# Earlier batch fronts and an earlier reciprocal in a two-layer attention and mixture-of-experts kernel

## The chip, the cores and the metric

The kernel runs on one core of a Trainium2 chip. The time is device microseconds of one execution, and the figure for the kernel before is the median of three executions: 1724.65 us (1723.31 to 1725.45). The profile is of one of them.

## The reference, cut to what matters

The input `x` has 4 batches of 1024 tokens of width 128. Two layers run one after the other, each as `x = x + layer(layernorm(x))`.

```
# layer 1: pre-norm attention, 16 heads of 8, causal, then a GELU MLP (128 -> 512 -> 128)
h = layernorm(x); q, k, v = h @ Wqkv; q, k = rotate(q), rotate(k)
a = softmax(where(causal, q @ k.T / sqrt(8), -inf)); x = x + (a @ v) @ Wo
x = x + gelu(layernorm(x) @ W1 + b1) @ W2 + b2
# layer 2: attention, 16 heads of 8, not causal, then 8 experts of which each token takes 2
q, k = rope(x @ Wq + bq), rope(x @ Wk + bk); v = x @ Wv + bv
ao = softmax(q @ k.T / sqrt(8)) @ v
x1 = layernorm(x + ao @ Wo + bo)
p = top2(softmax(x1 @ Wg + bg)), renormalised
out = layernorm(x1 + sum over the 2 experts of p_e * (gelu(x1 @ W1_e + b1_e) @ W2_e + b2_e))
```

## The kernel before, in words

Each engine has its own program, and semaphores tie the programs together. Both attentions are one class, `Attention`, with `a` = 1 (causal) and 2. The 64 pairs of batch and head are worked in 16 groups of 4 heads (`NG` = 16, `HG` = 4), so groups 0 to 3 are batch 0, 4 to 7 batch 1, and so on.

A group has two kinds of work. A **chunk** is one block of scores, made on TensorE (L536) only so that VectorE can take the row maxima of it (`row_max`, L623); there are 24 chunks in a group of the first attention and 32 in one of the second. A **unit** makes scores again (L568), now with the row maximum subtracted by extra rows of the operands, ScalarE takes the exponential (L677), and a **values** step (L592) multiplies it with V. There are 24 units in a group of the first attention and 32 in one of the second. A column of ones in V gives the sum of each row, and the sums leave with the outputs (`o_sums`, stored to DRAM as `heads_out`).

The order is written out once by `attention_plan` and every engine walks it: in group i, unit by unit, about one chunk is placed behind each unit, and those chunks belong to groups i+1 (chunks 6 and up) and, near the end, i+2 (chunks 0 to 5). All chunks share two PSUM buffers (`CHUNK_BUFS` = 2), so TensorE can be at most two chunks ahead of VectorE, and since the units stand between the chunks in the same program, whatever holds VectorE's row maxima soon holds TensorE and ScalarE.

When the four groups of batch b are done, the softmax sums of that batch are turned into reciprocals by three steps: SyncE reads the sums from DRAM into `sums_in` (`load_sums`, L469), in its turn for group i = 4(b+1), behind the row loads of a later group (`load`, L458, eight transfers); VectorE takes the reciprocal (`reciprocals`, L480); SyncE stores it (`store_reciprocals`, L473) in its turn for group i+1, again behind eight row loads. VectorE does its step in group i+1 (groups 5, 9, 13), two thirds of the way through the units (unit 16 of 24, unit 21 of 32). The step of the last batch stands elsewhere. Each SyncE turn i waits for all scores of group i before it issues the row loads.

In the second attention the **front** of a batch (output projection, layernorm, gate logits) is woven into a later group, `FRONT_GROUP[q]`: 7, 11 and 15 for batches 0, 1 and 2. SyncE loads its data before turn `FRONT_GROUP[q] - 1` (`load_front`, L982 to L985, three transfers for each half, after waiting for the stored reciprocals). GpSimd multiplies heads by reciprocals (`first_scale`, L1160), TensorE projects at `PRODUCT_UNIT` (L1329), VectorE adds and takes moments (L1572, L1555), ScalarE normalises 9 and 11 units later, TensorE transposes at `TURN_UNIT` (L762) and makes logits at `LOGITS_UNIT` (L1342). These TensorE steps borrow the chunk buffers. Group `SORT_GROUP` (12) holds the sort of tokens by expert for batches 0 and 1, and GpSimd scatters the tokens (L1191) from there on. Before turn 14 SyncE also loads the first three experts' weights (L1004) and the first sorted rows (L1016). After the attention come the expert blocks.

## Time and profile before

| | |
|---|---|
| median of three | 1724.65 us |
| the profiled execution, its own time | 1725.45 us |
| its span | 1723.6 us |
| TensorE busy | 1453.4 us (84%) |
| VectorE busy | 1275.0 us (74%) |
| ScalarE busy | 1164.6 us (68%) |
| first attention, group 0 to 15 | about 122 to 600 us of the span |
| second attention, group 0 to 15 | about 805 to 1471 us of the span |

In the names below PE is TensorE, PEld its weight load, DVE VectorE, ACT ScalarE, POOL GpSimd, and SPq the issuing queue of SyncE. An engine's idle time costs only where that engine, or one that waits for it, sets the pace.

### The profile page before, as it was taken

To read this page: it belongs to the slowest core of one execution; us is meant where nothing else is said; L and a number is where in the kernel's file an instruction comes from. 1 tells how busy PE (TensorE), PEld (TensorE's weight loads), DVE (VectorE), ACT (ScalarE), POOL (GpSimd) and SP (SyncE) were. 2 spreads that over 40 slices of the span, in tenths; PEclk is the share of its full clock that TensorE was granted. 3 is DMA by queue.
4 is the path that set the end of the run, shared out by engine and by line. 5 is a ranking of instruction groups with operands and counts; after the bars stand their busy time and mean duration, and the time that the engine had idled before them with its cause. 6 is when DMAs were issued, how large, how long until landed. Compare 5 with 4: busy or idle time off the path is not lost.

```text
span 1723.6 us, 39125 instructions
## 1 busy us (share of the span) xinstructions
PE 1453.4 (84%) x15249; PEld 668.5 (39%) x15249; DVE 1275.0 (74%) x1978; ACT 1164.6 (68%) x2370; POOL 370.9 (22%) x409
## 2 busy tenths in 40 slices
PE   4759999998989878856999999899988999898980
PEld 2323444444444355511222222222222223688870
DVE  6877787777777146569999999899989994261354
ACT  4627777777777755512989999789977998433341
POOL 3410000000000056420000000200021431267771
PEclk9959999999999989975999999999999999999995
DMA  3523241212111134440000102000200130566873
GB/s 115 189 84 113 94 139 56 78 53 85 57 46 36 62 102 129 128 140 8 33 33 33 39 34 71 33 32 34 71 32 34 64 124 14 156 189 212 265 227 104
DMA packets 132777, 152.94 MB, mean 89 GB/s; under 512 B 13744, under 2 KB 107824, under 8 KB 132336
## 3 DMA queue, kind: packets, MB, share of 16 engines
q1 hardware_dynamic: 122480, 123.43, 23.0%
q0 software_dynamic: 10112, 27.01, 4.2%
q8 instruction: 120, 1.97, 0.5%
q14 instruction: 65, 0.53, 0.1%
HBM read 90.90 MB, written 63.46 MB: 90 GB/s over the span
## 4 chain that ended last, share of the span: by engine, by line
PE 46%; DVE 25%; ACT 9%; issue 8%; DMA 6%; SPq 4%; POOL 2%; ACTq 0%; POOLq 0%; DVEq 0%
DVE row_max L623 20%; PE bank L592 16%; PE banks L568 9%; PE banks L536 6%; ACT probs L677 4%; PE banks L1386 4%; PE banks L1396 4%; DMA qk_parts<-parts 2%; SPq L486 2%; DMA q_work<-max_T 2%; PE banks L576 1%; ACT max_T L668 1%; ACT o_sums L688 1%; PE banks L323 1%; POOL pair_out L1202 1%
## 5 line engine op out<-in xcount | busy, mean ns | idle before, releaser
L623 DVE TENSOR_REDUCE row_max<-banks 128x2 f32<-128x1024 f32 (+3 forms) x896 | 938.1, 1101 | 130.7 <-PE banks L542 75.4
L677 ACT ACTIVATE probs<-banks 128x512 f32<-128x512 f32 (+3 forms) x1792 | 879.8, 552 | 175.8 <-PE banks L576 84.3
L592 PE MATMUL bank<-probs,v_ones 128*32 128x256 f32 (+3 forms) x7168 | 534.1, 375 | 20.0 <-ACT o_sums L688 16.8
L536 PE MATMUL banks<-k_work,q_work 48*128 48x512 bf16 (+3 forms) x1792 | 365.6, 380 | 75.8 <-DVE row_max L623 59.4
L568 PE MATMUL banks<-q_work,k_work 51*128 51x512 bf16 (+3 forms) x1792 | 384.5, 371 | 41.3 <-DMA q_work<-max_T 25.7
L715 POOL DMA_DIRECT2D heads_out<-o_sums x64 | 35.5, 555 | 1051.5 <-ACT o_sums L688 1051.5
L568 PEld LDWEIGHTS banks<-q_work,k_work 51*128 51x128 bf16 x1792 | 102.5, 93 | 407.7 <-ACT probs L677 316.7
L592 PEld LDWEIGHTS bank<-probs,v_ones 128*32 128x32 f32 x7168 | 147.1, 109 | 253.2 <-ACT probs L677 187.1
L536 PEld LDWEIGHTS banks<-k_work,q_work 48*128 48x128 bf16 x1792 | 95.0, 96 | 142.1 <-DVE row_max L623 108.4
L1962 ACT ACTIVATE rope<-banks,expert 128x256 f32<-128x256 f32 x184 | 72.0, 473 | 111.9 <-PE banks L1386 111.9
L1386 PE MATMUL banks<-rope,expert 128*128 128x256 f32 x368 | 93.2, 399 | 15.3 <-issue 7.7
L1396 PE MATMUL banks<-expert,rope 128*128 128x128 f32 x736 | 91.5, 278 | 0.6 <-DVE k_work L1699 0.6
L323 PE MATMUL banks<-hT,w_qk 128*128 128x512 f32 x128 | 69.5, 677 | 22.3 <-ACT hT L386 12.8
L1396 PEld LDWEIGHTS banks<-expert,rope 128*128 128x128 f32 x736 | 87.7, 195 | 0.8 <-ACT rope L1962 0.8
L576 PE MATMUL banks<-later_keys_T,half_ident 64*128 64x64 bf16 (+1 forms) x1024 | 80.3, 213 | 0.0
L1386 PEld LDWEIGHTS banks<-rope,expert 128*128 128x128 f32 x368 | 69.8, 200 | 25.2 <-issue 14.2
L542 PE MATMUL banks<-later_keys,half_ident 64*128 64x64 bf16 (+1 forms) x1024 | 75.2, 214 | 0.0
L1191 POOL DMA_INDIRECT sorted_in<-v_all,slots x64 | 67.6, 1056 | 20.9 <-issue 19.2
L668 ACT ACTIVATE max_T<-banks 12x1024 bf16<-12x1024 bf16 x32 | 32.1, 1004 | 54.9 <-PE banks L552 54.9
L1691 DVE COPY rope<-banks 128x256 f32<-128x256 f32 x46 | 19.4, 421 | 60.8 <-PE banks L1375 60.8
L542 PEld LDWEIGHTS banks<-later_keys,half_ident 64*128 64x128 bf16 x1024 | 55.7, 101 | 16.3 <-issue 3.2
L688 ACT ACTIVATE o_sums<-bank 128x512 f32<-128x512 f32 x64 | 38.9, 608 | 32.5 <-PE bank L592 32.5
(204 smaller groups left out, 1156.7 us busy)
## 6 DMA issues: line engine op xcount, KB each, us to landing
expert<-expert_rows SPq DMA_DIRECT2D x46, 578.0 KB, 4.0
qk_parts<-parts SPq DMA_DIRECT2D x64, 256.0 KB, 3.4
heads_out<-o_sums POOLq DMA_DIRECT2D x64, 256.0 KB, 4.3
q_work<-qk_parts SPq DMA_DIRECT2D x64, 128.0 KB
k_work<-qk_parts SPq DMA_DIRECT2D x64, 128.0 KB
sorted_in<-zeros SPq DMA_DIRECT2D x4, 1472.0 KB, 12.4
parts<-sorted_in SPq DMA_DIRECT2D x22, 256.0 KB, 4.7
probs<-in_x SPq DMA_DIRECT2D x16, 256.0 KB, 4.0
```

What stands on the lines that cost most here:

```text
L323: pe.matmul(bank[QK_BANK + u % QK_BANKS], w_qk[a][:, i, :], hT[:, :], start=True, stop=True).then_inc(s["qk"], 1)
L536: last = pe.matmul(to[:, par, 0:width], q[r:r + M0, pair, qt * P:(qt + 1) * P], k[r:r + M0, pair, kh * G:kh * G + width], start=True, stop ...
L542: last = pe.matmul(to[:, par, width - P + c0:width], half_ident[r:r + HALF, half, :], later_keys[r:r + HALF, half, c0:P], start=False, sto ...
L568: last = pe.matmul(to[par][:, 0:G - c0], k[r:r + M1, pair, kt * P:(kt + 1) * P], q[r:r + M1, pair, qh * G + c0:(qh + 1) * G], start=True, ...
L576: last = pe.matmul(to[par][:, 0:c1], half_ident[r:r + HALF, half, :], later_keys_T[r:r + HALF, half, 0:c1], start=False, stop=half == 1)
L592: last = pe.matmul(bank[7][32 * j:32 * j + 32, c0 + part * w:c0 + (part + 1) * w], v_ones[i % QB][:, kt, j, :], prob_slots[:, (e + j) % RI ...
L623: dve.tensor_reduce(row_max[:, qt, 2 * pair:2 * pair + 2, kh], self.buf_of("chunk", g, c)[:, :, 0:width], AX.X, ALU.max).then_inc(s["chunk ...
L677: act.activation(prob_slots[:, e % RING, 0:width], banks46[:, e % EXP_BANKS, 0:width], ACT.Exp, scale=SCALE).then_inc(s["exps"], 1)
L1191: pool.indirect_dma_start(xs_d[section], bass.IndirectOffsetOnAxis(slots[:, section, i, tile:tile + 1], 0), x1s[:, JOINED * section + tile ...
L1386: last = pe.matmul(hidden(m, f), expert[:, m % W_BUFS, f * P:(f + 1) * P], xsT[:, m % 2, :], start=True, stop=True)
L1396: last = pe.matmul(bank[Y_BANK][:, side * P:(side + 1) * P], h_block[:, m % 2, f, side * P:(side + 1) * P], expert[:, m % W_BUFS, FF + f * ...
L1962: act.activation(h_block[:, m % 2, f, :], hidden(m, f), ACT.Gelu, bias=expert[:, m % W_BUFS, 2 * FF + f:2 * FF + f + 1]).then_inc(end["gel ...
```

## The change

Two things change. VectorE's `reciprocals` step is no longer taken at two thirds of groups 5, 9 and 13 of both attentions, but ahead of the first chunk of these groups. And in the second attention the fronts of batches 0 and 1 go from groups 7 and 11 to groups 6 and 10, five units later in the group (product at 11 for 6, turn at 25 for 20, logits at 30 for 25); the front of batch 2 stays in group 15 at its units. `SORT_GROUP` follows from 12 to 11. SyncE's `load_front` stays before turns 6, 10 and 14, since `FRONT_GROUP[q]` now stands where `FRONT_GROUP[q] - 1` stood; the three expert loads go from turn 14 to turn 13.

```diff
-FRONT_GROUP = tuple(HG * q + 2 * HG - 1 for q in range(FIRST))
+FRONT_GROUP = tuple(HG * q + HG + 2 for q in range(JOINED)) + (NG - 1,)
 SORT_GROUP = FRONT_GROUP[JOINED - 1] + 1
-PRODUCT_UNIT, TURN_UNIT, LOGITS_UNIT, RANKS_UNIT = (6, 6, 1), (20, 20, 13), (25, 25, 17), 8
+PRODUCT_UNIT, TURN_UNIT, LOGITS_UNIT, RANKS_UNIT = (11, 11, 1), (25, 25, 13), (30, 30, 17), 8
...
                 for i in range(-1, NG):
+                    if i % HG == 1 and i > 1:
+                        self.reciprocals(dve, i // HG - 1)
                     for what, ahead, n in self.order:
-                        if what == "unit" and i % HG == 1 and i > 1 and n == self.nu * 2 // 3:
-                            self.reciprocals(dve, i // HG - 1)
...
             def load_ahead(i):
                 for q in range(FIRST):
-                    if i == FRONT_GROUP[q] - 1:
+                    if i == min(FRONT_GROUP[q], NG - 2):
                         for k in range(HALVES):
                             load_front(q, k)
-                if i == NG - 2:
+                if i == NG - 3:
                     sp.wait_ge(mid["x_out"], 16 * GROUPS)
                     sp.wait_ge(rows_made, 16 * len(made))
                     for m in range(W_BUFS - 1):
                         load_expert(m)
+                if i == NG - 2:
                     for i in range(2):
                         load_rows(0, i)
```

VectorE's program around the start of group 5 of the first attention, before (the row maxima of group 4's turn and group 5's run together in the count, 6 + 17):

```order
L641 CAST max_parts<-max_rest 128x32
L643 TENSOR_TENSOR max_parts<-max_rest,max_parts 128x32
L623 TENSOR_REDUCE row_max<-banks 128x2 x23
L480 RECIPROCAL sums_rcp<-sums_in 128x128
L623 TENSOR_REDUCE row_max<-banks 128x2
```

The same place after the change:

```order
L641 CAST max_parts<-max_rest 128x32
L643 TENSOR_TENSOR max_parts<-max_rest,max_parts 128x32
L623 TENSOR_REDUCE row_max<-banks 128x2 x6
L480 RECIPROCAL sums_rcp<-sums_in 128x128
L623 TENSOR_REDUCE row_max<-banks 128x2 x18
```

The reciprocal has moved ahead of 17 row maxima; behind it now stand all chunks that VectorE does in group 5's turn up to the maxima step. The five other places are alike.

TensorE's program in group 6 of the second attention (+ is what is new there; L1330 is L1329 of before), with the place in group 7 from which the first product is gone:

```order
@@ -2846,4 +2846,6 @@
 L592 MATMUL bank<-probs,v_ones 32x256 x4
 L568 MATMUL banks<-q_work,k_work 128x512 x2
+L1330 MATMUL banks<-w_o,headsT 128x128 x4
+L1330 MATMUL banks<-w_o,hT 128x128 x4
 L536 MATMUL banks<-k_work,q_work 128x512 x2
 L592 MATMUL bank<-probs,v_ones 32x256 x4
@@ -2924,6 +2928,4 @@
 L592 MATMUL bank<-probs,v_ones 32x256 x4
 L568 MATMUL banks<-q_work,k_work 128x512 x2
-L1329 MATMUL banks<-w_o,headsT 128x128 x4
-L1329 MATMUL banks<-w_o,hT 128x128 x4
```

The two projections stand behind unit 11 of group 6 and ahead of the next chunk of it; they stood behind unit 6 of group 7.

SyncE's program around turn 13 of the second attention:

```order
@@ -467,4 +467,16 @@
 L458 DMA k_work<-qk_parts 16x1x2048
 L469 DMA sums_in<-heads_out 128x1x128
+L1003 TENSOR_LOAD block_expert
+L1003 ISA x2
+L1004 ISA
+L1004 DMA expert<-expert_rows 128x1156
```

One of three such expert loads is shown; they now follow the read of the sums, and stood behind the six transfers of `load_front` one turn later.

## Rows read from the trace of the kernel before

**Rows 1.** The page's first part: busy us (share), instructions of each engine.

```profile
PE 1453.4 (84%) x15249; PEld 668.5 (39%) x15249; DVE 1275.0 (74%) x1978; ACT 1164.6 (68%) x2370; POOL 370.9 (22%) x409
```

**Rows 2.** Busy time by stretch: us, engines, granted clock (PEclk), DMA share, GB/s.

```profile
270.80:302.10 31.30, 28.93 (x424) 12.93 (x424) 23.77 (x31) 22.55 (x51) 1.50 (x4) 0.89 0.22 68
333.10:361.80 28.70, 26.05 (x424) 12.14 (x424) 22.91 (x30) 22.52 (x51) 1.48 (x3) 1.00 0.18 60
1043.00:1082.00 39.00, 37.10 (x394) 10.20 (x392) 37.49 (x38) 35.73 (x67) 1.48 (x3) 1.00 0.25 78
```

**Rows 3.** Timeline of VectorE, groups 5, 9, 13 of both attentions: start, length, [idle before].

```profile
272.20 1.22 DVE L623 TENSOR_REDUCE row_max<-banks 128x2 f32<-128x1024 f32 x1 [1.36 <-PE banks L542]
...
393.31 4.97 DVE L623 TENSOR_REDUCE row_max<-banks 128x2 f32<-128x1024 f32 x5 [1.37 <-PE banks L542]
...
513.16 4.97 DVE L623 TENSOR_REDUCE row_max<-banks 128x2 f32<-128x1024 f32 x5 [1.31 <-PE banks L542]
...
1003.68 2.49 DVE L623 TENSOR_REDUCE row_max<-banks 128x2 f32<-128x1024 f32 x2 [0.20 <-PE banks L536]
...
1174.12 2.49 DVE L623 TENSOR_REDUCE row_max<-banks 128x2 f32<-128x1024 f32 x2 [0.20 <-PE banks L536]
...
1350.15 2.49 DVE L623 TENSOR_REDUCE row_max<-banks 128x2 f32<-128x1024 f32 x2 [0.20 <-PE banks L536]
```

**Rows 4.** Timeline of SyncE's issues: row loads and reads of the sums.

```profile
402.22 0.71 SPq L469 DMA_DIRECT2D sums_in<-heads_out  x1
...
1004.52 2.61 SPq L458 DMA_DIRECT2D k_work<-qk_parts  x4
...
1177.72 0.56 SPq L469 DMA_DIRECT2D sums_in<-heads_out  x1
```

**Rows 5.** The read of the sums by line: first attention, second attention, all eight.

```profile
L469 SPq DMA_DIRECT2D sums_in<-heads_out x3: 567/708/1007, 280.8 to 517.1; - x3
DMA to landing us min/median/max: 6.0/6.6/8.9
...
L469 SPq DMA_DIRECT2D sums_in<-heads_out x3: 562/567/906, 1007.2 to 1353.7; - x3
DMA to landing us min/median/max: 8.5/9.1/10.3
...
DMA to landing us min/median/max: 2.2/7.5/10.3
```

**Rows 6.** The reciprocal by line: ns min/median/max, first to last start.

```profile
L480 DVE RECIPROCAL sums_rcp<-sums_in x8: 937/941/954, 292.6 to 1476.3; 128x128 f32<-128x128 f32 x8
```

**Rows 7.** Timeline, front loads and first work: SyncE, landing of L985, GpSimd, TensorE.

```profile
1046.84 0.41 SPq L473 DMA_DIRECT2D reciprocals<-sums_rcp  x1
1058.69 0.59 SPq L985 DMA_DIRECT2D xa<-z_d  x1
1228.92 0.59 SPq L985 DMA_DIRECT2D xa<-z_d  x1
...
DMA to landing us min/median/max: 4.6/5.0/5.8
...
1085.02 1.27 POOL L1160 TENSOR_TENSOR hT<-heads_in 128x512 f32<-128x512 f32 x1
...
1054.92 0.39 PE L568 MATMUL banks<-q_work,k_work 51*128 51x512 bf16 x2
1088.88 1.16 PE L1329 MATMUL banks<-w_o,headsT 128*128 128x128 f32 x8
1225.36 0.39 PE L568 MATMUL banks<-q_work,k_work 51*128 51x512 bf16 x2
```

**Rows 8.** Timeline of TensorE in group 7, at unit 16.

```profile
1110.57 0.64 PE L592 MATMUL bank<-probs,v_ones 128*32 128x256 f32 x8 [1.84 <-ACT o_sums L688]
```

**Rows 9.** Timeline of TensorE at the first expert block, after an idle stretch.

```profile
1477.66 3.62 PE L1386 MATMUL banks<-rope,expert 128*128 128x256 f32 x8 [5.22 <-DVE rope L1691]
...
1482.06 1.96 PE L1386 MATMUL banks<-rope,expert 128*128 128x256 f32 x8 [0.56 <-issue]
```

## The prediction, made before the changed kernel ran

> **What bounds the kernel now.** I read the page's busy times first, then the busy time by stretch, then the timeline of VectorE and TensorE at the places that the diff names, and last the issues and landings of the transfers there. TensorE is busy 84% of the span, VectorE 74% [rows 1]; the shares hide that the two attentions have different limits. A group of the first attention takes 28.7 us when the granted clock is 1.00, with TensorE busy 26.0 of it and VectorE 22.9: TensorE and ScalarE set the pace, VectorE has some spare time. A group of the second takes 39 us with VectorE busy 37.5 and TensorE 37.1 [rows 2]: VectorE sets the pace and nothing has room. In both, the chunks tie the engines: two buffers, so a wait on VectorE reaches TensorE after two chunks, and through the units ScalarE. Nothing behind can be done early, so a wait there is paid in full.
>
> The reader is to see for each touched step when its data lands against when its engine gets to it. Before, the reciprocals stand late enough that no wait shows in the six groups.
>
> **Step 1, the reciprocal ahead of the first chunk.** The instruction itself costs 0.94 us wherever it stands [rows 6]. What it waits for is the read of the sums, and that is issued late: SyncE first waits for all scores of the group before, then issues eight row loads. In the second attention the last of these are still being issued at 1004.5, and the read goes out at 1007.2 [rows 4, 5]. It lands 8.5 to 10.3 us after its issue, in the first attention 6.0 to 8.9 us [rows 5]. VectorE would start on the first chunk of the same group at 1003.7 [rows 3]. So the wait is there in all six places.
>
> *First attention.* The issues are at 280.8, 402.2 and 517.1, with 6.0, 6.6 and 8.9 us to land; the sum of the three landing times is 1200.1 + 21.5 = 1221.6, whichever delay belongs to which. VectorE's first chunks start at 272.20, 393.31 and 513.16, together 1178.7 [rows 3 to 5]. The difference is 42.9 us. The reciprocal comes on top, 3 x 0.94 = 2.8, because the place it leaves had spare time and gives nothing back. From 45.7 I take 0.3 for each place, since the first chunks of a group, which now wait ready in the buffers, follow each other a little more closely. That makes 45 us. TensorE can work on for two chunks and three units, then it stands too, so the whole is on the path.
>
> *Second attention.* Issues at 1007.2, 1177.7 and 1353.7, together 3538.6, and 8.5 + 9.1 + 10.3 = 27.9 to land, so 3566.5; first chunks at 1003.68, 1174.12 and 1350.15, together 3528.0 [rows 3 to 5]. The difference is 38.5 us, about 12 to 14 for each place. The 0.94 us is paid here and saved at unit 21, where VectorE also sets the pace: nothing.
>
> Both together 83.5 us. The bound below is a read that lands as fast as the fastest of the eight, 2.2 us [rows 5]; then the waits shrink by 21.5 + 27.9 - 6 x 2.2 = 36.2 to 47.3. Above, the landings might be slower by a microsecond or so each, where transfers that stood elsewhere come near: about 90. I take the landings as measured, because SyncE's program up to that read is the same and the same row loads are ahead of it. The Trainium skill (DMA: Bandwidth & Descriptors, Anatomy of one DMA) gives a transfer a fixed cost of about 2.0 us and 436 GB/s for its bytes, for one that has nothing ahead of it; by it alone these 64 KB would land in some 2.2 us, and step 1 would cost 47. The trace agrees for the fastest read only and has 6.0 to 10.3 us for the six that matter, so I give that rule a rival's chance below and no more.
>
> **Step 2, the fronts in groups 6 and 10.** The loads of a front stand in the same turn of SyncE as before, but the consumer comes a group earlier. In group 6: the reciprocals' store is issued at 1046.8 behind eight row loads, SyncE waits for its landing, and the last of the six front loads is issued at 1058.7. L985 takes up to 5.8 us to land: 1064.5. GpSimd's second product takes 1.27 us: 1065.8 [rows 7]. Without a wait TensorE would end unit 11 of that group at 1055.3 and start the second half's projection a microsecond later, at 1056.3 (in group 7 the first half took 1.16 us) [rows 7]. So it would stand for 9.5 us. In group 10 unit 11 ends at 1225.7, the last load is issued at 1228.9 and lands some 4.9 us later (the four are 4.6 to 5.8), 1233.8; with 1.27 it is 1235.1 against 1226.7: 8.4 us [rows 7]. Together 17.9 us. Queued behind TensorE's wait are the next chunk and unit, so VectorE and ScalarE stand as well, and it is paid in full. Bounds: 0, if the loads get there in time, and about 25, if the borrowed chunk buffers cost more at the new place than at the old one.
>
> What is won here: in group 7 TensorE waited 1.84 us for `o_sums` at unit 16, since ScalarE had been given the normalising between unit 15 and 17 [rows 8]. Now that comes at units 20 and 22 and is clear of it. Two fronts, 1.8 each: -3.6 us; between 0 and, if turn and logits also fall better, -7. The sort in group 11 is the same work in another group, and the scatter behind it starts a group earlier, with nobody waiting for it in either place. The expert loads in turn 13 go behind the read of the sums and have some 30 us until anyone wants the queue: 0, with a microsecond of slower landing as the worst, which is in the 90 above.
>
> **Step 3, the clock after the waits.** An idle TensorE comes back slowly: after 5.22 us idle the eight matmuls of L1386 took 3.62 us, the next eight 1.96 [rows 9]. That ratio of 1.85 is near that of the levels 1.2 and 2.4 GHz, and the price is 1.7 us. Five places of the second attention and three of the first have longer idle stretches than that. 8 x 1.7 = 13.6 us. Bounds: 0, and 2.6 us each (a group at a granted clock of 0.89 takes 31.3 us where one at 1.00 takes 28.7 [rows 2]), 21 us. The Trainium skill (TensorE: Matmul & The Clock Gate, What's actually happening) says that the default state is throttled and activity releases the throttle; by it each wait is followed by a slow start, as I count it. The trace differs in one way: the first attention falls to 0.89 in groups with no such idle stretch, so some of the slow stretches may only change place there, and without a cost for the three waits of the first attention the sum would be 5.1 us lower.
>
> **The sum.** 45 + 38.5 + 17.9 - 3.6 + 13.6 = 111.4 us. The profiled execution took 1725.45 us, 0.8 above the median of the three: 1725.45 + 111.4 = 1836.9, said as 1837 us.
>
> **The rivals.**
>
> *The fronts' loads are in time.* If the long waits at the start of groups 5 and 9 let the transfers run ahead, group 6 and 10 would find their data. Against it: SyncE's turns are tied to the scores of the same groups, so they are late by the same amount. Without the 17.9 and the two slow starts (3.4) the time is 1815.6, about 1816 us.
>
> *The sums land fast.* While VectorE waits the core is quiet, and the read of 64 KB could land near 2.2 us. For it: the fastest of the eight did [rows 5]. Against it: the row loads ahead of it are the same. Then 36.2 less: 1801 us.
>
> *Faster than before.* The gain of step 2 is real (3.6 us), and if the reciprocals cost nothing and the fronts' data were there, it would be all: 1725.45 - 3.6 = 1722 us. It decides for this side only where the read of the sums has landed by the time VectorE ends the group before, which is some 14 us earlier than any of the six did [rows 3, 5]. I see nothing that would bring that.
>
> *Dearer.* The two chunk buffers are lent to the fronts near the transposes of the row maxima, at the end of the group. If each of turn and logits then waits for a max_T copy, and the clock takes 2.6 us after each wait, it is 1837 + 7 + 8 = 1852 us or a little more.
>
> **How the numbers follow.** The forecast, with step 1, 2 and 3 as worked out: 0.72. Loads of the fronts in time: 0.10. Sums land fast: 0.06. Dearer: 0.09. Faster than before: 0.02; something between that and the others, such as no change because both waits are hidden: 0.01. The range is from 1806 (a forecast without any slow start and with -7 for the relief is 1820; the free fronts with cheaper starts reach down to 1806) to 1856 (the dear case). About 0.2% is what a measurement can tell from no change, 3.5 us. Faster 0.02, same 0.01, slower 0.97.
>
> **What would show it.** In the profile after, VectorE's idle time before the reciprocal (L480) goes to about 120 us over eight places, six of them of 12 to 17 us and ended by the read of the sums. TensorE idles once each in groups 6 and 10 before the projections, for 8 to 10 us, ended by GpSimd's product. The `o_sums` wait of 1.84 us is gone from the groups with a front. Slices with a granted clock below 1 follow each wait in the second attention, which has almost none now. The stretch from the end of the second attention to the end keeps its length. It would be wrong if the waits before L480 were under 8 us each, or if TensorE idled in groups 5, 9 and 13 without the length of the group growing.

## The result and the profile after

| | before | changed |
|---|---|---|
| median | 1723.98 us (4 runs) | 1848.99 us (4 runs, 1845.05 to 1852.15) |
| the profiled execution, its own time | 1725.45 us | 1848.04 us |
| its span | 1723.6 us | 1846.2 us |

The ratio is 1.0728, 95% interval 1.0699 to 1.0758: 125 us slower, where 111 were forecast.

First the page of the changed kernel, busy time by engine:

```profile
PE 1478.0 (80%) x15249; PEld 671.7 (36%) x15249; DVE 1278.0 (69%) x1978; ACT 1164.4 (63%) x2370; POOL 372.5 (20%) x409
```

VectorE and ScalarE did the same work as before [rows 1] to 3 us; TensorE's 25 us more is the same 15249 matmuls, some of them at the lower clock level. Of the 122.6 us that the span grew, VectorE was therefore idle for all but 3, and TensorE for 98. The waits of the changed kernel, who waited for whom, us in total, times, longest:

```profile
DVE sums_rcp L480 <- DMA sums_in<-heads_out: 107.2, 8, 18.8
```

Of these 107.2 us, 18.8 and 0.8 belong to the last batch of each attention, where the kernel before waited about as long (18.7 us for the two). The other six make 87.6. Where VectorE meets them, in group 5 of the first attention and of the second (start, length, [idle before]), which answers to [rows 3]:

```profile
270.45 1.82 DVE L623 TENSOR_REDUCE row_max<-banks 128x2 f32<-128x768 f32 x2 [0.17 <-PE banks L542]
288.78 0.95 DVE L480 RECIPROCAL sums_rcp<-sums_in 128x128 f32<-128x128 f32 x1 [16.51 <-DMA sums_in<-heads_out]
289.65 3.42 DVE L623 TENSOR_REDUCE row_max<-banks 128x2 f32<-128x1024 f32 x3
...
1049.27 3.49 DVE L623 TENSOR_REDUCE row_max<-banks 128x2 f32<-128x1024 f32 x3 [0.40 <-PE banks L536]
1065.24 0.95 DVE L480 RECIPROCAL sums_rcp<-sums_in 128x128 f32<-128x128 f32 x1 [12.48 <-DMA sums_in<-heads_out]
1066.11 3.42 DVE L623 TENSOR_REDUCE row_max<-banks 128x2 f32<-128x1024 f32 x3
1069.96 1.23 DVE L623 TENSOR_REDUCE row_max<-banks 128x2 f32<-128x1024 f32 x1 [0.43 <-PE banks L536]
1071.51 1.22 DVE L623 TENSOR_REDUCE row_max<-banks 128x2 f32<-128x1024 f32 x1 [0.33 <-PE banks L536]
```

The reader is to see two things. The reciprocal starts within 0.1 us of its data, 12 to 17 us after VectorE was free. And behind it the row maxima run on with under a microsecond of idle time: two chunks stood ready in the buffers, and TensorE's slow start shows on VectorE as small gaps only. TensorE at the same place:

```profile
1067.33 0.61 PE L536 MATMUL banks<-k_work,q_work 48*128 48x512 bf16 x2 [12.38 <-DVE row_max L623]
1067.87 1.08 PE L592 MATMUL bank<-probs,v_ones 128*32 128x256 f32 x8
1068.88 0.61 PE L568 MATMUL banks<-q_work,k_work 51*128 51x512 bf16 x2
1069.28 0.64 PE L536 MATMUL banks<-k_work,q_work 48*128 48x512 bf16 x2
1069.85 1.08 PE L592 MATMUL bank<-probs,v_ones 128*32 128x256 f32 x8
1070.86 0.39 PE L568 MATMUL banks<-q_work,k_work 51*128 51x512 bf16 x2
1071.09 0.38 PE L536 MATMUL banks<-k_work,q_work 48*128 48x512 bf16 x2
...
1072.19 0.38 PE L536 MATMUL banks<-k_work,q_work 48*128 48x512 bf16 x2
```

The eight matmuls of L592 take 1.08 us and not 0.64, the pair of L568 0.61 and not 0.39, until 1070.9; so TensorE worked at the lower clock level for about 3.5 us. From one chunk (L536) to the next it took 1.95 and 1.81 us there and 1.10 after, so this start cost it about 1.5 us.

The issue and the landing of the read, first three of the first attention, then of the second (answers to [rows 5]):

```profile
L469 SPq DMA_DIRECT2D sums_in<-heads_out x3: 566/713/1007, 282.2 to 550.7; - x3
DMA to landing us min/median/max: 6.3/6.6/8.5
...
L469 SPq DMA_DIRECT2D sums_in<-heads_out x3: 557/563/567, 1056.5 to 1458.9; - x3
DMA to landing us min/median/max: 8.7/9.0/11.5
```

Now the front in group 6: SyncE's issues, GpSimd, TensorE, VectorE (answers to [rows 7]):

```profile
1109.63 0.42 SPq L473 DMA_DIRECT2D reciprocals<-sums_rcp  x1
1118.90 0.57 SPq L982 DMA_DIRECT2D heads_in<-heads_out  x1
...
1124.91 1.26 POOL L1161 TENSOR_TENSOR headsT<-heads_in 128x512 f32<-128x512 f32 x1 [17.57 <-DMA heads_tok<-z_d]
1127.24 1.26 POOL L1161 TENSOR_TENSOR hT<-heads_in 128x512 f32<-128x512 f32 x1 [1.07 <-DMA xa<-z_d]
...
1126.32 2.04 PE L1330 MATMUL banks<-w_o,headsT 128*128 128x128 f32 x8 [8.31 <-POOL headsT L1161]
1128.56 2.07 PE L1330 MATMUL banks<-w_o,hT 128*128 128x128 f32 x8 [0.20 <-POOL hT L1161]
...
1128.40 0.69 DVE L1573 TENSOR_TENSOR xz<-banks,heads_tok 128x512 f32<-128x512 f32 x1 [9.69 <-PE banks L1330]
1130.67 0.69 DVE L1573 TENSOR_TENSOR yT<-banks,xa 128x512 f32<-128x512 f32 x1 [1.58 <-PE banks L1330]
```

SyncE waits 9 us for the store of the reciprocals, the loads land, GpSimd multiplies, TensorE has stood 8.3 us and then does both projections at the lower clock level, 2.04 us each and not 1.16 and 1.06. VectorE is idle 11.3 us, for TensorE's two projections; in group 7 of the kernel before these two waits were 0.74 us. In group 10 TensorE stood 7.1 and 0.4 us, and the projections took 2.05 and 1.87.

Both stretches by time, groups 5 and 6 of the second attention (from:to, length, PE, PEld, DVE, ACT, POOL busy, granted clock, DMA share, GB/s); [rows 2] has a group of 39 us at 1.00:

```profile
1052.50:1105.50 53.00, 38.91 (x394) 10.28 (x392) 38.51 (x39) 35.87 (x67) 1.48 (x3) 0.87 0.08 28
1105.50:1169.40 63.90, 48.93 (x434) 17.12 (x432) 43.14 (x62) 39.87 (x78) 11.61 (x13) 0.87 0.16 50
```

Measured from one group's last `o_sums` copy to the next, the difference between the two kernels splits like this:

| stretch | before | changed | more |
|---|---|---|---|
| first attention, groups 5, 9, 13 | 88.4 | 136.8 | 48.4 |
| the rest up to the end of the first attention | 510.0 | 509.3 | -0.7 |
| up to the end of group 0 of the second | 248.1 | 249.6 | 1.5 |
| second attention, groups 5, 9, 13 | 119.0 | 163.0 | 44.0 |
| groups 6 to 8 (front of batch 0) | 130.8 | 144.3 | 13.5 |
| groups 10 to 12 (front of batch 1, sort) | 136.4 | 151.5 | 15.1 |
| everything else | 491.1 | 491.8 | 0.7 |

### The profile page after: what moved, and what is told of

The parts are those of the page before. It is cut to its first block, busy times and chain, and to the rows that moved or that the text cites. A ratio compares the mean times of both kernels' runs of the same rounds, so it can differ in the third digit from the quotient of the medians.

```text
span 1846.2 us, 39125 instructions
## 1 busy us (share of the span) xinstructions
PE 1478.0 (80%) x15249; PEld 671.7 (36%) x15249; DVE 1278.0 (69%) x1978; ACT 1164.4 (63%) x2370; POOL 372.5 (20%) x409
## 4 chain that ended last, share of the span: by engine, by line
PE 43%; DVE 21%; issue 9%; DMA 9%; ACT 8%; SPq 7%; POOL 2%; ACTq 0%; POOLq 0%; DVEq 0%
DVE row_max L623 16%; PE bank L592 15%; PE banks L568 9%; PE banks L536 6%; PE banks L1387 4%; PE banks L1397 3%; ACT probs L677 3%; DMA sums_in<-heads_out 3%; SPq L486 3%; SPq L458 2%; DMA qk_parts<-parts 2%; DMA q_work<-max_T 1%; ACT max_T L668 1%; PE banks L576 1%; ACT o_sums L688 1%
## 5 line engine op out<-in xcount | busy, mean ns | idle before, releaser
L592 PE MATMUL bank<-probs,v_ones 128*32 128x256 f32 (+3 forms) x7168 | 546.0, 383 | 16.7 <-ACT o_sums L688 13.6
L536 PE MATMUL banks<-k_work,q_work 48*128 48x512 bf16 (+3 forms) x1792 | 370.2, 387 | 156.2 <-DVE row_max L623 140.9
L568 PE MATMUL banks<-q_work,k_work 51*128 51x512 bf16 (+3 forms) x1792 | 390.1, 376 | 44.9 <-DMA q_work<-max_T 25.7
L568 PEld LDWEIGHTS banks<-q_work,k_work 51*128 51x128 bf16 x1792 | 102.9, 93 | 422.1 <-ACT probs L677 327.2
L592 PEld LDWEIGHTS bank<-probs,v_ones 128*32 128x32 f32 x7168 | 148.8, 110 | 262.6 <-ACT probs L677 189.1
L536 PEld LDWEIGHTS banks<-k_work,q_work 48*128 48x128 bf16 x1792 | 95.4, 97 | 220.2 <-DVE row_max L623 189.9
L480 DVE RECIPROCAL sums_rcp<-sums_in 128x128 f32<-128x128 f32 x8 | 7.6, 953 | 107.2 <-DMA sums_in<-heads_out 107.2
```

Source lines behind the costliest of these rows:

```text
L536: last = pe.matmul(to[:, par, 0:width], q[r:r + M0, pair, qt * P:(qt + 1) * P], k[r:r + M0, pair, kh * G:kh * G + width], start=True, stop ...
L568: last = pe.matmul(to[par][:, 0:G - c0], k[r:r + M1, pair, kt * P:(kt + 1) * P], q[r:r + M1, pair, qh * G + c0:(qh + 1) * G], start=True, ...
L592: last = pe.matmul(bank[7][32 * j:32 * j + 32, c0 + part * w:c0 + (part + 1) * w], v_ones[i % QB][:, kt, j, :], prob_slots[:, (e + j) % RI ...
```

## The experiments

The kernels of one set ran on one chip beside the kernel before. The three sets (e1 to e4, e5 to e8, e9 to e12) met three chips, on which the kernel before took 1815.8, 1732.7 and 1731.1 us. Each result is given against the kernel before of its own set; where an expectation names an absolute time, it stands on 1724 us, and its difference to the kernel before is what counts.

### e1, the reciprocal alone

```diff
 # the kernel before, with
+                    if i % HG == 1 and i > 1:
+                        self.reciprocals(dve, i // HG - 1)
                     for what, ahead, n in self.order:
-                        if what == "unit" and i % HG == 1 and i > 1 and n == self.nu * 2 // 3:
-                            self.reciprocals(dve, i // HG - 1)
```

> The kernel before with the reciprocal alone moved ahead of the first chunk of groups 5, 9 and 13 of both attentions; fronts and expert loads stay. My theory: the six waits for the read of the sums are paid in full and add up with the front's cost, so this alone is worth 88 to 95 us (six waits of 12 to 17 us before L480, 89 us of idle time in the changed kernel, and at most 1 us for each slow start): about 1816 us. Rival (part of the wait is only shifted into the fronts: whatever waits at group 5 is saved at group 6): the sum of the two halves alone is clearly more than 125 us, so this one is over 1830 or the fronts alone cost under 15 us.

1907.33 against 1815.76 us: ratio 1.0508 (1.0453 to 1.0562), 91.6 us more by the medians. VectorE waited 101.6 us before L480, 16.9 of them at the end. As expected.

### e2, the fronts alone

```diff
 # the changed kernel, with
-                    if i % HG == 1 and i > 1:
-                        self.reciprocals(dve, i // HG - 1)
                     for what, ahead, n in self.order:
+                        if what == "unit" and i % HG == 1 and i > 1 and n == self.nu * 2 // 3:
+                            self.reciprocals(dve, i // HG - 1)
```

> The changed kernel with the reciprocal put back at two thirds of the group: only fronts, sort and expert loads are moved. My theory: the late front loads hold TensorE 9 to 11 us in groups 6 and 10, the projections run at the lower clock level after it (about 2 us each) and nothing is won back: 24 to 30 us more than before, about 1751 us. Rival (the forecast's smaller term, 14.3 us net and 3.4 us of slow start): about 1742 us. Rival (the fronts wait only because the reciprocals came late): no wait here, 1720 us.

1839.11 against 1815.76 us: ratio 1.0151 (1.0093 to 1.0208). By the medians 23.4 us more, just under my 24 to 30; the interval (17 to 38 us) holds the forecast's smaller figure of 17.7 as well, so the total alone does not tell the two apart. The trace does, on the point of the wait: TensorE stood 7.3 us before the projections of group 6, and both ran at 2.05 us. The third theory falls: the reciprocals were ready in time here, and the fronts waited all the same. The two halves together are 5.1 + 1.5 = 6.6%, against 6.5% and 7.3% for the whole: they add.

### e3, the read of the sums ahead of the row loads

```diff
 # the changed kernel, SyncE's turn i
                     if i + QB < NG:
                         sp.wait_ge(self.s["scores"], (i + 1) * self.ne)
+                    if i % HG == 0 and i:
+                        self.load_sums(sp, i // HG - 1)
+                    if i + QB < NG:
                         self.load(sp, i + QB)
                     if between:
                         between(i)
-                    if i % HG == 0 and i:
-                        self.load_sums(sp, i // HG - 1)
```

> The changed kernel with one move on SyncE: the read of the sums is issued ahead of the eight row loads (and, in the first attention, of the weight copies) of the same turn instead of behind them. My theory: the read lands late because of what is queued ahead of it, so it is issued 5 to 10 us earlier and lands in 2 to 3 us; VectorE's waits before L480 fall from 12 to 17 us to under 2 us each, and the time falls by about 85 us to 1764 us, with the fronts' 28 us still there. Rival (the landing is slow by itself, 6 to 10 us, whatever is ahead of it): the waits fall only by the earlier issue, 5.4 us in the second attention and 10 in the first, 45 us in all: about 1804 us.

1847.15 against 1815.76 us: ratio 1.0185 (1.013 to 1.024). The changed kernel itself did not run on this chip; against the sum of the halves, 115 us, that is 84 less. What is left, 31.4 us, is the fronts' 23.4 and the six waits that remain, 7.9 us together. The same read in the second attention, issue and landing, and VectorE at group 5:

```profile
L469 SPq DMA_DIRECT2D sums_in<-heads_out x3: 592/597/602, 1011.2 to 1409.2; - x3
DMA to landing us min/median/max: 2.2/2.3/2.7
```

```profile
1013.43 0.95 DVE L480 RECIPROCAL sums_rcp<-sums_in 128x128 f32<-128x128 f32 x1 [0.56 <-DMA sums_in<-heads_out]
```

The landing falls from 8.7 to 11.5 us to 2.2 to 2.7, by nothing but its place in the queue. So each wait of the second attention had two parts: SyncE's eight issues (5.4 us), and 6 to 9 us by which the read landed later behind those loads. In the first attention the first part was the larger one: in the first of the three places the read went out 10.4 us earlier against the start of its turn, since copies of weights stood ahead of it too, and it landed in 2.3 us in all three, where it had taken 6.3 to 8.5. Whether it is the bytes of the loads or their number that holds the read was not tried.

### e4, the new units in the old groups

```diff
-PRODUCT_UNIT, TURN_UNIT, LOGITS_UNIT, RANKS_UNIT = (6, 6, 1), (20, 20, 13), (25, 25, 17), 8
+PRODUCT_UNIT, TURN_UNIT, LOGITS_UNIT, RANKS_UNIT = (11, 11, 1), (25, 25, 13), (30, 30, 17), 8
```

> The kernel before with the new units (product 11, turn 25, logits 30) in the old groups 7 and 11, so that no load is late. It prices the place inside the group. My theory: the wait for o_sums at unit 16 goes (1.8 us in each group), but ScalarE's normalising and the turn now hold the chunks at units 20 to 28 instead, so the net is between -2 and +3 us: 1722 to 1727. Rival (the forecast's gain of 3.6 us): 1720 us. Rival (the borrowed chunk buffers near the maxima's transposes are dear, which would explain why the fronts cost 10 us more than forecast): 1730 us or more.

1815.8 against 1815.76 us (medians; one of the ten executions took 4927 us, for no known reason): ratio 1.0009 (0.9984 to 1.0033). The place in the group is worth nothing that can be told (3 us less to 6 us more); the gain of 3.6 us that the forecast counted is not there. In the changed kernel the 1.84 us wait of [rows 8] is indeed down to 0.43, but VectorE now idles 1.18 and 1.11 us at units 20 and 22, where ScalarE's normalising went. TensorE, then VectorE, in group 6:

```profile
1144.48 0.64 PE L592 MATMUL bank<-probs,v_ones 128*32 128x256 f32 x8 [0.43 <-ACT o_sums L688]
...
1150.37 2.36 DVE L623 TENSOR_REDUCE row_max<-banks 128x2 f32<-128x1024 f32 x2 [1.18 <-PE banks L536]
1153.84 1.22 DVE L623 TENSOR_REDUCE row_max<-banks 128x2 f32<-128x1024 f32 x1 [1.11 <-PE banks L536]
```

### e5, the changed kernel again

> The changed kernel itself, beside the three kernels below and the kernel before on one chip. The first four experiments ran where the kernel before takes 1816 us and not 1724. My theory: the extra time there lies behind the scatter of group 12, which is common to all kernels, and the change costs about the same there: 115 us (the halves alone cost 91.6 and 23.4 us) to 125 us more than the kernel before on the same chip, whichever this is. Rival (the change and the slow stretch add to each other): over 140 us.

1847.43 against 1732.67 us: ratio 1.0649 (1.0613 to 1.0685), 115 us more. So the cost of the change is between 6.5 and 7.3% by chip. The rival of an interplay is not tested by it, since the kernel before was not slow on this chip (1732.67 us); what speaks against it is that the halves came to 115 us together where the kernel before took 1816.

### e6, read and store first

```diff
 # the changed kernel, SyncE's turns
                 for i in range(NG - 1):
+                    if i % HG == 0 and i:
+                        self.load_sums(sp, i // HG - 1)
+                    if i % HG == 1 and i > 1:
+                        self.store_reciprocals(sp, i // HG - 1)
                     if before:
                         before(i)
...
-                    if i % HG == 0 and i:
-                        self.load_sums(sp, i // HG - 1)
-                    if i % HG == 1 and i > 1:
-                        self.store_reciprocals(sp, i // HG - 1)
```

> The changed kernel, with the read of the sums and the store of the reciprocals issued at the very start of SyncE's turns 4(b+1) and 4(b+1)+1, ahead of the row loads, the copies of the maxima and the front loads; the reciprocal stays ahead of the first chunk, the fronts stay in groups 6 and 10. My theory: the read lands a whole group before VectorE wants it, so no wait before L480, and the front loads are issued some 8 us earlier (about 3 us into group 6, landing by 10 us), so TensorE waits at most 2 us at unit 11: the time is within 5 us of the kernel before on the same chip. Rival (fronts in groups 6 and 10 cost by themselves, 20 us or more, even with their data there): 20 us or more above it.

1752.33 against 1732.67 us: ratio 1.0111 (1.008 to 1.0142). The waits before L480 are gone, but it is 20 us slower and not 5: my expectation failed, and the total looks like the rival's. The trace says why, SyncE and TensorE in group 6:

```profile
1047.52 2.60 SPq L458 DMA_DIRECT2D k_work<-qk_parts  x4
1050.30 0.56 SPq L982 DMA_DIRECT2D heads_in<-heads_out  x1
...
1055.09 0.60 SPq L985 DMA_DIRECT2D xa<-z_d  x1
...
1065.31 2.05 PE L1330 MATMUL banks<-w_o,headsT 128*128 128x128 f32 x8 [6.64 <-POOL headsT L1161]
```

The front loads were issued 9 us earlier (4 us into group 6, and not 13), but now directly behind the row loads, and GpSimd could start on the last of them only 10.9 us after its issue (1055.1 to 1066.0). The 9 us wait for the store in the changed kernel had been the same queue: whoever stands behind the row loads pays for them, the store or the loads. That left two theories, so a further experiment issued these loads a turn earlier, ahead of those row loads (e9, below).

### e7, the same for the old fronts

The kernel before with the early reciprocal and SyncE's order of the last experiment.

> The kernel before (fronts in groups 7 and 11, old units) with the reciprocal ahead of the first chunk, and the read and the store issued first as in the kernel beside it. My theory: no wait is left, so it is within 3 us of the kernel before; the early place of the reciprocal is harmless once its data is there. Rival (an instruction of 0.94 us ahead of the first chunk costs by itself, since TensorE's first chunks and the maxima chain are delayed, or the earlier read holds up SyncE): 6 us or more slower.

1729.97 against 1732.67 us: ratio 0.9997 (0.9972 to 1.0022). The early reciprocal costs nothing once its data is there.

### e8 and e10, keeping TensorE busy in the wait

```diff
 # the changed kernel; TensorE, ahead of the third chunk of groups 5, 9, 13 of the second attention
+WARM = 45
...
+                def warm(i):
+                    e = i * self.ne + 2 * 3
+                    pe.wait_ge(s["exps"], e - EXP_BANKS + 1)
+                    for _ in range(WARM):
+                        pe.matmul(banks46[:, e % EXP_BANKS, :], k_rows[i % QB][0:M1, 0, 0:P], q_rows[i % QB][0:M1, 0, 0:G],
+                                  start=True, stop=True)
...
                         if what == "chunk" and i + ahead < NG:
+                            if self.a == 2 and i % HG == 1 and i > 1 and (ahead, n) == (1, LEAD + 2):
+                                warm(i)
```

> The changed kernel, in which TensorE fills its wait in groups 5, 9 and 13 of the second attention with 45 extra matmuls of 512 columns (about 10 us at the higher clock level) into a score bank that is free then; nothing else is changed and their result is overwritten. It measures what the slow start behind a wait costs. My theory after the result: about 1 us a wait (these groups grew 13.4, 13.8 and 16.7 us where the wait grew 12.5, 12.8 and 15.4), so 3 us less than the changed kernel. Rival (the price of the forecast, 1.7 us a wait): 5 us less. Rival (the slow start costs nothing behind a full pair of buffers, the extra is something else): 0.

1858.29 against 1732.67 us, 11 us more than the changed kernel beside it: none of the three. The extra matmuls were slow themselves:

```profile
1054.69 17.08 PE L603 MATMUL banks<-q_work,k_work 51*128 51x512 bf16 x43
```

```profile
1054.00:1066.00 12.00, 11.79 (x32) 4.17 (x32) 1.20 (x2) 1.61 (x4) 0.00 (x0) 0.59 0.23 88
```

The first seven or eight ran at the higher level (granted clock 1.00 from 1054.6 to 1056.2 us); from 1056.2 on the granted clock was 0.50 and one started every 0.43 us, with TensorE busy all the time. So they ended after VectorE's wait and made the three groups longer: 58.8 to 58.9 us, where the changed kernel beside it took 54.0 to 57.8. A second try used pairs, one in each half of the array rows, as the kernel's own scores are made:

```diff
-WARM = 45
+WARM = 26
...
-                    pe.wait_ge(s["exps"], e - EXP_BANKS + 1)
-                    for _ in range(WARM):
-                        pe.matmul(banks46[:, e % EXP_BANKS, :], k_rows[i % QB][0:M1, 0, 0:P], q_rows[i % QB][0:M1, 0, 0:G],
-                                  start=True, stop=True)
+                    pe.wait_ge(s["exps"], e + 1 - EXP_BANKS + 1)
+                    for _ in range(WARM):
+                        for par in range(2):
+                            r = par * HALF
+                            pe.matmul(banks46[:, (e + par) % EXP_BANKS, :], k_rows[i % QB][r:r + M1, 0, 0:P],
+                                      q_rows[i % QB][r:r + M1, 0, 0:G], start=True, stop=True)
```

> The changed kernel with 26 pairs of extra matmuls (both halves of the array rows, as the kernel's own scores have them) in TensorE's wait in groups 5, 9 and 13 of the second attention. The 45 single matmuls of e8 took 18 us instead of 10, so they ran over the wait and the group grew; 26 pairs end inside it at either level (some 6 or 11 us). If TensorE now keeps the higher level, groups 5, 9 and 13 are shorter than in the changed kernel (53 to 58 us) by what the slow start costs. My theory: about 1 us each, 3 us less in all. Rival (forecast): 1.7 us each, 5 us. Rival (an engine kept busy with such work is slow all the same): no gain, and the pairs take some 11 us.

1847.88 against 1731.05 us: ratio 1.0668 (1.064 to 1.07), no gain on the changed kernel (1.0649, 1.0728).

```profile
1057.93 5.79 PE L605 MATMUL banks<-q_work,k_work 51*128 51x512 bf16 x52 [0.59 <-ACT probs L689]
1069.79 0.61 PE L537 MATMUL banks<-k_work,q_work 48*128 48x512 bf16 x2 [6.08 <-DVE row_max L635]
1070.32 1.08 PE L593 MATMUL bank<-probs,v_ones 128*32 128x256 f32 x8
```

The pairs ran at the higher level, 0.22 us a pair, but left 6 us of idle time, and TensorE came back slow after it all the same. So neither run kept it at the higher level to the end of the wait, and the price of the slow start was not measured by itself; what bounds it is the growth of the groups (below).

### e9, the front loads early too

```diff
 # the kernel of "read and store first", with
-                    if i == min(FRONT_GROUP[q], NG - 2):
+                    if i == FRONT_GROUP[q] - 1:
```

> Read of the sums and store of the reciprocals first, as in e6, and in addition the front loads one turn earlier (before turns 5, 9 and 14, while fronts are in groups 6, 10 and 15). In e6 TensorE still waited in group 6, since the six front loads were issued behind the eight row loads of turn 5 and landed 9 us later. My theory: the whole cost of the change is lateness of transfers, so with these out of the way the fronts in groups 6 and 10 cost what they cost in 7 and 11, and the time is that of the kernel before, within 5 us (group 6 about 51 us long, where it was 64). Rival (the new place costs by itself): 10 us or more above the kernel before, with group 6 at 56 us or more.

1733.86 against 1731.05 us: ratio 1.0014 (0.9994 to 1.0034). SyncE issues the front loads at 1012.8 to 1016.0, a turn earlier, and TensorE in group 6 has no wait ahead of the projections, which are at their full speed:

```profile
1012.75 0.57 SPq L982 DMA_DIRECT2D heads_in<-heads_out  x1
...
1015.97 0.59 SPq L985 DMA_DIRECT2D xa<-z_d  x1
...
1051.78 1.16 PE L1330 MATMUL banks<-w_o,headsT 128*128 128x128 f32 x8
1052.77 1.06 PE L1330 MATMUL banks<-w_o,hT 128*128 128x128 f32 x8
```

Group 6 is 53.8 us long, between my 51 and the rival's 56, and inside what group 7 took in kernels that keep the front there (50.7 to 58.1 us). With this the changed places are all there and the cost is gone: nearly all of it was lateness of transfers, with the slow starts behind the waits. This version is the best with the new places, and it is no faster than the kernel before.

### e11, the fronts later in the group

```diff
 # the fronts alone, with
-PRODUCT_UNIT, TURN_UNIT, LOGITS_UNIT, RANKS_UNIT = (11, 11, 1), (25, 25, 13), (30, 30, 17), 8
+PRODUCT_UNIT, TURN_UNIT, LOGITS_UNIT, RANKS_UNIT = (16, 16, 1), (28, 28, 13), (31, 31, 17), 8
```

> The fronts alone in groups 6 and 10 (reciprocals at two thirds of the group, as before the change), with the product at unit 16 instead of 11, turn at 28 and logits at 31. My theory: TensorE's wait is the lateness of the front loads, so five units later (5.6 us) it is shorter by about that, from some 10 to 4 us for each front, and the kernel is 12 to 15 us slower than the kernel before, where the fronts at unit 11 were 23.4 us slower. Rival (the cost is in the place, near the maxima and the transposes, not in the loads): no less than 23 us slower.

1741.73 against 1731.05 us: ratio 1.0055 (1.0027 to 1.0082), 10.7 us more, a little under the 12 to 15. TensorE's wait before the projections of group 6 is 3.29 us, where the fronts at unit 11 (e2) had 7.29 and, for the second half, 0.67. The projections still ran at the lower level, 2.04 and 2.07 us.

### e12, the expert loads alone

```diff
 # the kernel before, load_ahead
-                if i == NG - 2:
+                if i == NG - 3:
...
                         load_expert(m)
+                if i == NG - 2:
```

> The kernel before with the three expert loads issued one turn of SyncE earlier, nothing else. The forecast gave this 0. In the changed kernel the read of the sums of batch 2 took 11.5 us to land instead of 10.3. My theory: 0 here, since nobody waits for that read at two thirds of the group. Rival (1.7 MB in the way of the copies of the maxima): 2 us or more slower.

1731.27 against 1731.05 us: ratio 0.9998 (0.9975 to 1.0021). Nothing, as forecast.

## Why the prediction was right, by its own steps

**Step 1** was forecast at 83.5 us, and with the slow starts of its six waits from step 3 (10.2) at 93.7. The two attentions' groups 5, 9 and 13 grew 48.4 and 44.0 us, 92.4 in all; the kernel with this step alone was 91.6 us slower. The mechanism is shown from both sides: with the step alone the cost is there, with the read ahead of the row loads the waits fall to 0.6 to 2.1 us, and with read and store first it is gone. VectorE's waits are 47.0 us in the first attention and 40.6 in the second, but not all of that is new: in the kernel before it had already stood, ahead of its first chunk, 1.36, 1.37 and 1.31 us, and 0.20 three times [rows 3]. The new part is 43.0 and 40.0 us, where 42.9 and 38.5 were forecast. Of the landings in the second attention the forecast took 8.5, 9.1 and 10.3 us; the last one came to 11.5 in the changed kernel. The expert loads stand right behind that read since the change. In the kernel in which they alone were moved the read took 10.9 us (e12), so they may account for half a microsecond of it; these are single readings.

One reading behind this step was not right: a group of the first attention has ScalarE busy 22.5 us and VectorE 22.9 [rows 2], so by these rows TensorE alone sets the pace there, and ScalarE has as much spare time as VectorE. Nothing in the sum hangs on it.

**Step 2** was forecast at 17.9 - 3.6 = 14.3 us, with its two slow starts at 17.7, and is where the sum was off: the groups with it grew 13.5 and 15.1, together 28.6 us. The wait itself was nearly right: in group 6 TensorE stood 8.3 + 0.2 us where 9.5 were forecast, in group 10 7.1 + 0.4 where 8.4 were. The projections ran slow right after it, 4.11 us for the two and not 2.2, as step 3 had it. The relief of 3.6 us does not exist: the new units measure 1.0009 (0.9984 to 1.0033) by themselves, since the normalising that no longer delays `o_sums` delays the scores of two later units instead. What was counted as a gain was a wait that moved. The waits on TensorE (8.5 us, and 7.5 in group 10) and the two slow pairs of projections (1.9 and 1.7) make 19.6 of the 28.6 us.

The other 9 us are on TensorE too, and are mostly its clock. Here are the two groups that hold a front, in the profiled execution of five kernels; only the last one has late loads:

| kernel | length, us | granted clock | TensorE busy, us |
|---|---|---|---|
| before, groups 7 and 11 | 50.7, 50.7 | 1.00, 1.00 | 43.0, 43.0 |
| e7, groups 7 and 11 | 58.2, 52.1 | 0.85, 0.97 | 50.5, 44.4 |
| e12, groups 7 and 11 | 55.2, 58.2 | 0.91, 0.85 | 47.7, 50.5 |
| e9, groups 6 and 10 | 53.8, 54.3 | 0.90, 0.91 | 47.3, 47.6 |
| changed, groups 6 and 10 | 63.9, 64.7 | 0.87, 0.84 | 48.9, 50.5 |

A front's group takes 50.7 us at a granted clock of 1.00 and 58.2 at 0.85, in kernels in which nothing in it is late and whose times are those of the kernel before. The forecast stood on an execution in which both had 1.00, and gave slow work to the waits only. So part of these 9 us may have come without the change; how much, and what lowers the clock in these groups, is open.

**Step 3** was forecast at 13.6 us, 1.7 for each of eight waits. In groups 5, 9 and 13 of the second attention the growth is 44.0 us and the new waits are 40.0: 4.0 us are left, 1.3 each. The timeline above, by which one start cost TensorE about 1.5 us, fits with it. The price of [rows 9] was taken where TensorE has no chunks ready and VectorE waits for every matmul; that here the two chunks in the buffers hide a part is a reading of the timeline and was not tested. In the first attention the growth is 48.4 us, the new waits 43.0 and the reciprocals 2.8, which leaves 2.6 for three. That figure is loose: a group there takes 28.6 or some 31.2 us, at granted clocks of 1.00 and 0.89, and which ones are slow changes from one execution to the next without any wait. Group 5 took 31.2 us in the profile before and 28.6 in those of e2, e4, e9, e11 and e12. Against 28.6 the three starts would have cost 5.2. So the six slow starts behind the reads came to somewhere between 0.9 and 1.7 us each, and with the projections' 3.6 us all eight came to 10 to 13 us.

The rest of the 122.6 us, about 1.5, lies between the attentions and behind the second, where the same work varies by more than that between kernels (the stretch up to group 0 of the second attention took 244 to 250 us).

So the forecast was right in its mechanism and in most of its terms. It came out 11 us low: the relief (3.6) and the clock of the fronts' groups (9) were missing, the waits for the reads were some 2 us too low, and against them stood slow starts and fronts' waits that were taken some 3 and 2 us too high. That is within its range; that errors of both signs partly cancel is luck. VectorE's idle time before L480 is 107.2 us over the eight places, where the signs to look for said about 120.

Of the rivals, *the fronts' loads are in time* failed because SyncE's turn shifts with the group, as was said against it. *The sums land fast* is what the read does when it is issued first: 2.2 to 2.7 us in e3. The figures that the forecast takes from the Trainium skill (DMA: Bandwidth & Descriptors, Anatomy of one DMA) are given there for transfers that GpSimd issues; SyncE's read agrees with them only with no row loads ahead of it. The forecast was right to keep the measured landing, since the row loads stayed ahead of it. *Dearer* named 1852 us, and the 1849 measured are nearer to that than to 1837. Its mechanism is not what happened: in group 6 TensorE has no wait right ahead of the turn and the logits, the new units alone cost nothing (e4), and with early loads the new places cost nothing either (e9). *Faster than before* had nothing for it: no wait was hidden.

## What to carry to other kernels

Before a step is moved earlier, look up when its data lands, not when it is issued: in the second attention 64 KB behind eight row loads took four times as long as the same 64 KB ahead of them. If the consumer is to move, move the producer first, and with it each link of the chain; of read, store and front loads, moving the first two took 95 us of the cost away (1847 to 1752 us), and the last one 17 of the remaining 20. A wait that a move removes is a gain only if the work that caused it has not been put in front of another wait. And before a small term is priced, look at how the same group does in several executions: the fronts' groups took 50.7 to 58.2 us with nothing in them late, at granted clocks of 1.00 to 0.85.

## What the hardware showed that was not expected

TensorE kept busy with single matmuls on 51 of the 128 rows fell to the lower clock level 1.5 us after they began and stayed there (granted clock 1.00 to 1056.2 us, 0.50 from there to 1071), while the same matmuls as pairs in both halves of the rows kept the higher one for the 5.8 us that they lasted (26 pairs in 5.79 us, granted clock 1.00). The singles also wrote one PSUM bank and the pairs two in turn; which of the two differences counts was not tried.

On one of the chips the kernel before took 1815.8 us where it takes 1724 to 1733 elsewhere. In the run there with the new units in the old groups, which is as fast as it, group 11 of the second attention ends at 1303.7 us, as on the first chip (1303.2), and groups 12 and 13, in which GpSimd scatters the sorted rows, take longer. Group 12, then group 13 there:

```profile
1303.70:1358.70 55.00, 43.73 (x411) 12.43 (x409) 44.47 (x83) 36.26 (x68) 12.30 (x12) 0.91 0.10 35
1358.70:1416.50 57.80, 45.38 (x394) 10.74 (x392) 39.52 (x39) 36.09 (x68) 16.97 (x19) 0.82 0.13 45
```

The same groups took 46.5 and 39.7 us on the first chip, with busy times on VectorE, ScalarE and GpSimd within 1 us of these. VectorE has waits there of up to 4.4 us for things that the profile does not name. The cause is open.
